# A four-stage graph network on one core: the two graph convolutions with a ring of 24 tile groups and loops over two step groups

## The reference, cut to what matters

```python
def gcn_conv(x, src, dst, W, b, n_nodes):
    deg = jax.ops.segment_sum(ones, dst, num_segments=n_nodes)
    dinv = jnp.where(deg > 0, jax.lax.rsqrt(jnp.maximum(deg, 1.0)), 0.0)
    norm = dinv[src] * dinv[dst]
    h = x @ W
    out = jax.ops.segment_sum(h[src] * norm[:, None], dst, num_segments=n_nodes)
    return out + b
h = jax.nn.relu(gcn_conv(x, src, dst, W1, b1, n))
return gcn_conv(h, src, dst, W2, b2, n)
```

## Time and profile before

| | us |
|---|---|
| median of three runs | 15079.31 |
| profiled execution | 14940.95 |
| its span | 14939.1 |
| first layer | 0 to about 3,300 |
| second layer | about 3,400 to 7,500 |
| third layer | about 7,600 to 10,130 |
| convolution 0, loops | 10209.5 to 12523 |
| convolution 1, loops | 12552 to 14861 |

### The profile page before, as it was taken

The page is one execution under the profiler, slowest core; times in us unless marked ns, Lnnn a source line. Parts: engine busy times, 40 slices in busy tenths (PEclk is TensorE's granted clock), DMA queues, the critical chain, the costliest instruction groups (busy, mean ns, idle before and its releaser), DMA issues.

```text
span 14939.1 us, 182194 instructions
## 1 busy us (share of the span) xinstructions
PE 8307.1 (56%) x46670; PEld 7582.8 (51%) x46671; DVE 6695.0 (45%) x13205; ACT 2723.1 (18%) x6542; POOL 8996.6 (60%) x8046
## 2 busy tenths in 40 slices
PE   5777787765555555578845555563333334333334
PEld 5777777754445444477745554463333333333333
DVE  6444444434444444489945565564222223222223
ACT  0111111101111111266623333340000000000000
POOL 3888888873556655500037777754666664666664
PEclk7666666666666667799967677775555555555555
DMA  4333333332333333332212222221111111111111
GB/s 91 18 18 18 18 18 18 18 51 68 97 96 98 98 99 96 99 100 98 94 47 66 66 68 67 67 65 27 23 23 23 23 23 26 23 23 23 23 23 23
DMA packets 851085, 769.36 MB, mean 51 GB/s; under 512 B 652784, under 2 KB 660804, under 8 KB 848965
## 3 DMA queue, kind: packets, MB, share of 16 engines
q0 software_dynamic: 446272, 333.87, 16.1%
q1 hardware_dynamic: 249485, 294.83, 5.9%
q10 hardware_dynamic: 155282, 140.11, 3.1%
HBM read 569.49 MB, written 197.82 MB: 51 GB/s over the span
## 4 chain that ended last, share of the span: by engine, by line
issue 23%; another core or an unknown queue 19%; PE 18%; POOL 15%; DVE 10%; DMA 8%; DVEq 5%; ACT 1%; ACTq 0%; POOLq 0%; SPq 0%
POOL lane_tab L679 9%; DMA lane_tab<-rows,idx 7%; POOL tab L703 6%; PE ps L1127 3%; PE ps L1153 3%; PE ps L1128 3%; DVEq L469 2%; DVE acc_w L1797 2%; DVEq L458 1%; DVE buf_d L469 1%; PE ps L1192 1%; PE ps L1178 1%; PE ps L1168 1%; PE ps L1113 1%
## 5 line engine op out<-in xcount | busy, mean ns | idle before, releaser
L703 POOL DMA_INDIRECT tab<-gcn_tab,idx x3136 | 2983.1, 951 | 1807.3 <-issue 1232.9
L679 POOL DMA_INDIRECT lane_tab<-rows,idx x1664 | 2598.3, 1561 | 616.8 <-issue 616.8
L703 POOL DMA_INDIRECT tab<-att_tab,idx x1568 | 1739.2, 1109 | 1923.1 <-DVEq L1684 1311.1
L1168 PE MATMUL ps<-tab,buf_d 128*128 x3328 | 795.2, 387 | 2162.6 <-issue 2121.8
L1168 PEld LDWEIGHTS ps<-tab,buf_d 128*128 128x128 f32 x3328 | 781.0, 320 | 2249.3 <-issue 2249.3
L1797 DVE TENSOR_TENSOR acc_w<-acc_w,ps 128x512 f32 x416 | 286.1, 688 | 3395.9 <-remote 3108.7
L693 POOL DMA_INDIRECT buf_b<-src_tab,idx x832 | 825.6, 992 | 749.4 <-ACT idx L813 296.4
L693 POOL DMA_INDIRECT acc_w<-src_tab,idx x832 | 838.0, 1007 | 598.0 <-ACT idx L813 335.1
L1065 PE MATMUL ps<-ident,srcg 128*128 128x128 f32 x3328 | 721.9, 405 | 659.6 <-DVE srcg L1430 655.1
L1168 PE MATMUL ps<-tab,buf_a 128*128 x3328 | 762.8, 424 | 531.7 <-issue 403.3
L1168 PEld LDWEIGHTS ps<-tab,buf_a 128*128 128x128 f32 x3328 | 725.9, 330 | 650.5 <-issue 650.1
(11 more groups left out here) (283 smaller groups left out, 16942.2 us busy)
## 6 DMA issues: line engine op xcount, KB each, us to landing
y_stash<-buf_c SPq DMA_DIRECT2D x208, 512.0 KB
tab<-y_stash SPq DMA_DIRECT2D x208, 512.0 KB, 3.3
aux<-dst_rows ACTq DMA_DIRECT2D x104, 512.0 KB
buf_b<-dst_rows ACTq DMA_DIRECT2D x104, 512.0 KB
tab<-gcn_tab,idx POOLq DMA_INDIRECT x3136
aux<-in_edge_attr_dram ACTq DMA_DIRECT2D x848, 32.0 KB
aux<-in_edge_attr_dram SPq DMA_DIRECT2D x848, 32.0 KB
lane_tab<-rows,idx POOLq DMA_INDIRECT x1664
```

The costliest lines, as they stand in the source:

```text
L679: pool.indirect_dma_start(lane_tab[k][:, :], bass.IndirectOffsetOnAxis(ap=idx[:, b, u:u + 1], axis=0), rows[:, b, u, 0:D1], None, compute_ ...
L703: pool.indirect_dma_start(to[k][:, u, :], None, table[:, :], bass.IndirectOffsetOnAxis(ap=idx[:, k % RING, u:u + 1], axis=0)).then_inc(row ...
L1168: last = pe.matmul(ps_flat[:, bass.ds(rel[u] + q * 512, D)], g_hot[q][:, u, :], g_ring[:, bass.ds(at[u], D)], start=False, stop=True, skip ...
```

## The change

The ring gets 24 slots (so AHEAD becomes 24 - 13 = 11). 24 slots of 512 floats fill most of `tab`, so the places move to `buf_b` in a shorter form (nine integers a step group: eight ring places and the needed tile groups), and the eight places in PSUM are read from `rel_s`, which is scaled in place. TensorE then loads registers twice a step group (`load8` and the new `load_tiles`). A ring of 24 is no power of two, so the place in the ring is worked out by VectorE with a multiplication, a shift and a multiply-add on the row `g_turn` in `buf_c`. Both loops run 104 times (ITER) over two step groups, with two one-hots and two banks. VectorE's order within a turn changes: it waits for the sum of step group g, adds it, frees the bank, and only then writes the one-hot of step group g + 2 into the buffer that step group g has just left. GpSimd's loop body becomes 24 tile groups long.

```diff
-LONG = 16
+LONG = 24
...
-        g_places = tab_flat[0:1, PLACES_AT:PLACES_AT + S // G * GP].bitcast(I32)
-        g_hot = [buf_a[:, 0, :, :], buf_a[:, 1, :, :], buf_d[:, 0, :, :], buf_d[:, 1, :, :]]
+        g_places = buf_b[:, :, :, :].rearrange("p a b c -> p (a b c)")[0:1, 0:S // G * (G + 1)].bitcast(I32)
+        g_turn = buf_c[:, :, :, :].rearrange("p a b c -> p (a b c)")[0:1, 0:S].bitcast(I32)
+        g_hot = [buf_a[:, 0, :, :], buf_a[:, 1, :, :]]
...
+        def load_tiles(g):
+            _, v = nc.values_load_multi_w_load_instructions(
+                g_places[:, bass.ds(g * (G + 1), G + 1)], engines=(mybir.EngineType.PE,), min_val=0, max_val=(LONG * G - 1) * D,
+                skip_runtime_bounds_check_because=PLACES_WHY)
+            return v[0:G], nc.s_assert_within(v[G], RING + 1, RING * (TT + 1))
...
             def aggregate(left_ready, landed, free, done):
-                with pe.Fori(0, TURNS) as i:
-                    for q in range(RING):
-                        g = i * RING + q
+                with pe.Fori(0, ITER) as i:
+                    for q in range(2):
+                        g = i * 2 + q
...
-                        rel, at, needed = load_steps(g)
+                        rel = load8(mybir.EngineType.PE, rel_s, g, (G - 1) * D)
+                        at, needed = load_tiles(g)
...
-            link(dve.tensor_scalar(row_s[:, 0:S], row_s[:, 0:S], LONG * G - 1, None, ALU.bitwise_and))
-            link(dve.tensor_scalar(g_steps[:, :, G:2 * G], row_grp, float(D), None, ALU.mult))
-            link(dve.tensor_scalar(g_steps[:, :, 0:G], rel_grp, float(D) / P, None, ALU.mult))
+            link(dve.tensor_scalar(g_turn, row_s[:, 0:S], 683.0, None, ALU.mult))
+            link(dve.tensor_scalar(g_turn, g_turn, 17, None, ALU.arith_shift_right))
+            link(dve.scalar_tensor_tensor(g_turn, g_turn, -float(LONG * G), row_s[:, 0:S], ALU.mult, ALU.add))
+            link(dve.tensor_scalar(g_steps[:, :, 0:G], g_turn.rearrange("p (a u) -> p a u", u=G), float(D), None, ALU.mult))
+            link(dve.tensor_scalar(rel_s[:, 0:S], rel_s[:, 0:S], float(D) / P, None, ALU.mult))
...
-                dve.sem_inc(bank_free, RING)
+                dve.sem_inc(bank_free, 2)
                 dve.sem_inc(outs, AHEAD)
                 for g in range(2):
                     one_hot_by_step(dve, g_hot[g], g).then_inc(hot, 1)
-                with dve.Fori(0, TURNS) as i:
-                    for q in range(RING):
-                        g = i * RING + q
-                        dve.wait_ge(outs, g + (AHEAD - 1))
-                        one_hot_by_step(dve, g_hot[(q + 2) % RING], g + 2).then_inc(hot, 1)
+                with dve.Fori(0, ITER) as i:
+                    for q in range(2):
+                        g = i * 2 + q
                         w0 = load1(mybir.EngineType.DVE, win_s, g, W - 1)
                         dve.wait_ge(outs, g + (AHEAD + 1))
                         a = acc_w[:, bass.ds(w0, G), 0:D]
...
                         dve.wait_ge(order, g + 2)
                         dve.sem_inc(bank_free, 1)
+                        one_hot_by_step(dve, g_hot[q], g + 2).then_inc(hot, 1)
```

More of the change, by code:

```diff
@@ L64 @@
 GP = 2 * G + 1
-PLACES_AT = LONG * G * D2
 ZEROS = 195
@@ L69 @@
 EPS = 1e-5
-assert 0 < AHEAD and LREST == RING and L2_RING % RING == 0 and all((t * 1639) >> 18 == t // (L2_RING * G) for t in range(T8)) and L2_RING * G * D2 + S <= 2 * W * D and 2 * G * P + S // G * GP <= W * D1 and PLACES_AT + S // G * GP + 2 * P <= 2 * W * D and WPP * PAIRS == W and LONG * G == P and TURNS * RING * G == S and SPAD == S + RING * G and SB == TB and CHUNKS * WPC == W and PAIRS * WPP == W and CHUNKS % 2 == 0 and ITER % 2 == 0 and ITER * PAIR == S and CH <= 512 and SROWS * D1 // P % ZEROS == 0
+assert 0 < AHEAD and LREST == RING and L2_RING % RING == 0 and all((t * 1639) >> 18 == t // (L2_RING * G) for t in range(T8)) and L2_RING * G * D2 + S <= 2 * W * D and 2 * G * P + S // G * GP <= W * D1 and LONG * G * D + P <= 2 * W * D and S // G * (G + 1) <= 2 * G * P and all((t * 683) >> 17 == t // (LONG * G) for t in range(T8)) and WPP * PAIRS == W and TURNS * RING * G == S and SPAD == S + RING * G and SB == TB and CHUNKS * WPC == W and PAIRS * WPP == W and CHUNKS % 2 == 0 and ITER % 2 == 0 and ITER * PAIR == S and CH <= 512 and SROWS * D1 // P % ZEROS == 0
 def build(nc, x, src, dst, ea16, ea64, w_edge, b_edge, w_node, b_node,
@@ L434, in build, with load_steps @@
         PLACES_WHY = "the table's entries are made from clamped step places"
-        def load_steps(g, places=g_places, stride=P // 2, n=D, ring=LONG):
+        def load_tiles(g):
[3 more added lines that the diff above has]
+            return v[0:G], nc.s_assert_within(v[G], RING + 1, RING * (TT + 1))
+        def load_steps(g, places, stride, n, ring):
             _, v = nc.values_load_multi_w_load_instructions(
@@ L1647, in _ @@
             dve.sem_inc(s.l2_windows, 1)
-            l2_steps, g_steps = (t.rearrange("p (a k) -> p a k", k=GP) for t in (l2_places, g_places))
+            l2_steps = l2_places.rearrange("p (a k) -> p a k", k=GP)
+            g_steps = g_places.rearrange("p (a k) -> p a k", k=G + 1)
             row_grp = row_s[:, 0:S].rearrange("p (a u) -> p a u", u=G)
@@ L1652, in needed_tiles @@
             def needed_tiles(steps):
-                needed = steps[:, :, 2 * G:GP]
+                n = steps.shape[2]
+                needed = steps[:, :, n - 1:n]
                 link(dve.tensor_scalar(needed, row_grp[:, :, G - 1:G], G.bit_length() - 1, None, ALU.arith_shift_right))
```

## The result

The changed kernel takes 15186.7 us (median of 9 runs, 15122.4 to 15211.2), the kernel before, measured beside it, 15077.1 us (9 runs, 15020.0 to 15083.6). The recorded ratio is 1.0086, 95% interval 1.0070 to 1.0102. That is a small loss, clear of the noise, where a gain was forecast (14420 us). The quotient of the two medians would be 1.0073. The ratios in this text are the recorded ones, and they can differ from the quotient of the medians by up to 0.3%. The profiled execution after has a span of 15184.8 us, 246 us above the one before, where the medians show 110 us. The stages say where the time lies.

A forecast was written before the change was run, and what follows sets the result against it. GpSimd's gathers and pauses were taken to bound the convolutions. 14941 - 668 (573 of it pauses) + 2 = 14275 us, plus 138 us from profiled execution to median, 14413, rounded to 14420 us; range 14380 to 15290 us.

The forecast's parts named there:

- What bounds the kernel: In the convolutions GpSimd always either gathers, one per 1.252 us, 1963 us a convolution, or pauses, 287 us.
- The ring of 24 as the gain: GpSimd's lead grows to 11 groups, 110 us of gathers, outlasting the 31.5 us hand-over delay; 573 us of pauses go.
- The third layer: Earlier stage with as many gathers, lead of seven groups, only 122.2 us of pauses; evidence against gathering itself slowing the hand-over.
- The tail: After a convolution's last gather: TensorE has only one or two step groups left, 14 us in place of 69.5.
- Two register loads: TensorE's second load per step group adds 1.4 us, making 7.2 us, hidden by the 10.0 us of a tile group.
- Two banks and two one-hots: TensorE's hand-over to VectorE in the convolutions may be 10 us late at no cost; delays of 19 and 31 uncovered.
- Rival D: Two banks lock TensorE to the gathering-dependent delay: three groups a turn, 35.8 us, +196 us, 15275 us; chance 0.32.
- Loop turns and setup: 104 more taken branches in the convolution loops cost zero; setup's three row operations become five, +2 us.
- A: The forecast itself: convolution hand-over delay does not grow, GpSimd gathers without pause; 14420 us, chance 0.40.

The follow-up runs named there:

- e1: Kernel before with the ring of 24 alone, with its table and second register load; 13329.7 us, ratio 0.9988, session without pauses.
- e4: Changed kernel with a GpSimd wait, before each tile group's fourth gather, for the previous tile group's rows; 13343.2 us, ratio 0.9996, session without pauses.
- e10: Changed kernel (ring of 24) with six banks, six one-hots and loops over six step groups; 14977.1 us, ratio 1.0042, session with pauses.
- e3: Kernel before with a GpSimd wait, before each tile group's fourth gather, for the previous tile group's rows; 13333.7 us, ratio 0.9987, session without pauses.
- e11: Kernel before with loops over two step groups, two one-hots and two banks alone, ring of 16; 14957.2 us, ratio 1.0041, session with pauses.
- e5: The changed kernel, unmodified, measured again beside the kernel before; 15038.6 us, ratio 1.0110, session with pauses.
- e7: Kernel before with loops over two step groups, two one-hots and two banks alone, same kernel as e2; ratio 1.0005, session without pauses.
- e2: Kernel before with loops over two step groups, two one-hots and two banks alone, ring of 16; 13337.6 us, ratio 0.9990, session without pauses.
- e13: Kernel before with a step group's one-hots written by one 128x1024 VectorE operation instead of eight; 13423.3 us, ratio 1.0050, session without pauses.
- e14: Kernel before with GpSimd waiting, ahead of each tile group, for the previous one's rows; ratio 1.0584, session without pauses.
- e16: Kernel before with GpSimd waiting, ahead of every second tile group, for the previous one's rows; ratio 1.0304, session without pauses.
- e17: Same kernel as e16, in a session of its own, also without pauses; ratio 1.0321.

## Why the prediction was wrong, point by point

**What bounds the kernel: right.** GpSimd either gathers at 1.25 us or pauses. In the sessions without pauses the gathers of a convolution take 1962 to 1971 us in e1 to e4, against the 1963 of the sum.

**The ring of 24 as the gain: the step that failed.** The sentence was "If delays stay of that size, GpSimd never waits", and it took 573 us off the time; 637 us of pauses in the two convolutions are what the changed kernel has (320 + 317), where the kernel before has 570. It took the hand-over delay of 31.5 us as a length of time that a lead of 110 us outlasts. The runs with pauses show a delay without a length: of the additions that the turn hangs on, the last comes only when GpSimd has been silent for four to five and a half us (medians: 5.3 with a lead of 3, 4.4 in the changed kernel and 5.4 in e10 with a lead of 11), however far GpSimd is ahead. The lead is spent once, in the first 14 tile groups, and then every turn ends in a pause again: 62 and 61 pauses in the changed kernel, 47 a convolution in e10 with the same ring. The forecast read the earlier trace rows, where the addition starts "when GpSimd has been silent for about five us", and did not let it decide. The third layer, the row that spoke against it, was the wrong witness. Fewer pauses of GpSimd there say nothing of how late the counts come to the other engines. Two lines of the kernel before for that stage (7645 to 10130 us), which the earlier trace rows does not show, say that they come late there too; the third line is the same place of VectorE in e3 (6959 to 9162 us), without pauses:

```profile
ACT buf_d L901 <- remote: 739.5, 56, 105.0
DVE buf_c L1713 <- remote: 523.2, 30, 61.0
```

```profile
DVE buf_c L1720 <- PE ps L1244: 450.5, 138, 15.3
```

GpSimd's 21 pauses of the third layer (130 us) are gone in e3 and e1 as well, and its gathers take 2200 and 2204 us there in place of 2351.

**The tail: wrong in its sign.** I took 14 us for it in place of 69.5, since TensorE would follow the data. With pauses TensorE follows up to eleven tile groups behind, and has them all to do after the last gather: 137 us to the next convolution's first gather in place of 99.5, with six banks and the ring of 24 118, with the ring of 16 and two banks (e11) 113. Both halves of the change lengthen the tail, the ring somewhat more. Without pauses the stretch is 36 us (e1).

**Two register loads: too dear.** I took 7.2 us a step group. In the changed kernel's tail the matmuls of consecutive groups start at 12599.79, 12605.99, 12611.44, 12616.44 and 12620.52:

```profile
12599.79 3.67 PE L1175 MATMUL ps<-tab,buf_a 128*128 x16
...
12605.99 3.67 PE L1175 MATMUL ps<-tab,buf_a 128*128 x16 [2.09 <-issue]
...
12611.44 3.67 PE L1175 MATMUL ps<-tab,buf_a 128*128 x16 [1.36 <-issue]
...
12616.44 3.67 PE L1175 MATMUL ps<-tab,buf_a 128*128 x16 [0.90 <-issue]
...
12620.52 3.67 PE L1175 MATMUL ps<-tab,buf_a 128*128 x16
```

That is 20.73 / 4 = 5.2 us a group, as before over four groups (12480.33 to 12501.17 us, 20.84 / 4), where the forecast had 5.8: the loads of nine integers take 2.35 us (median) where that of 17 took 4.03, and the loads of eight 0.59 us.

```profile
L437 PEldq TENSOR_LOAD <-buf_b x416: 1021/2352/2368, 10292.5 to 15099.7; - x139
```

**Two banks and two one-hots: right as a mechanism, and it decided.** Rival D had named it with the right place (TensorE's clearing matmul waiting for VectorE), the right point (a delay above 10 us; 20.4 us are seen) and the right count (three groups a turn). Its price a tile group was 11.95 us, measured 34.75 / 3 = 11.58, since the pause is 5.0 us and takes the place of one gap of 0.3: 3 x 10.0 + 4.7 against the 35.8 written. The larger error is the pause, which D took as long as before. Against 11.46 before that is 0.12 x 392 = 47 us where D had 196; in e11, which has this part alone, the gathers show 2 x 16 us. D left out the longer tail, 2 x 38 us, of which e11 shows 2 x 12. The whole change has a ratio of 1.0086, and 1.0110 in e5; the loops alone have 1.0041, the ring with six banks 1.0042. That the two halves about add up is no proof, since the ring with four banks was never measured with pauses and each interval is wide.

**Loop turns and setup:** nothing in the rows speaks against the zero and the 2 us; e7 and e2, with twice the turns and no pauses, are within 0.3% of before.

**Chances.** D had 0.32 and A 0.40. The range of 14380 to 15290 us holds the 15187 measured, but only because it was drawn to take in the nearer half of D; the forecast itself has the wrong sign and is 767 us too low. What should have turned them round is that the earlier trace rows show the same late addition at the same distance from GpSimd's last gather in turns of different content, while A rested on an analogy with another layer.

**What stays open.** Why the counts and TensorE's matmuls are held back while GpSimd gathers, and only in some sessions, is not settled. Neither a longer lead (e10, the changed kernel) nor more than four banks and one-hots (e10) removes it. Whether fewer instructions or short silences would free them was not seen, since e13, e14, e16 and e17 fell in sessions without pauses, nor whether a shorter queue of gathers would (e3, e4); what the ring alone does with pauses is known only from the change and from e10. No version measured beats both kernels in both kinds of session: with prompt counts all variants of ring, loops and banks are equal within 0.3%, with late ones the kernel before is the fastest of the four that were measured.

## What to carry to other kernels

Ask of a late hand-over what ends it before you buy slack against it: if each one ends at a fixed distance from another engine's silence, a longer lead only moves the silence, and lengthens the tail. When an engine's results are seen late, count the buffers between it and its reader first: two banks and two one-hots fewer turned four groups a turn into three here. And measure beside the old kernel in more than one session: a difference that one session shows can be nothing in another.

## What the runs showed of the hardware

The same kernel took 14890 to 15080 us in some sessions and 13320 to 13380 us in others at the same granted TensorE clock (0.64 to 0.65 as a mean over the span). In the convolutions the difference is whether counts of finished groups are seen at once (e1: VectorE's addition behind the matmuls, no "remote" wait of GpSimd) or late (by 20.4 us in the changed kernel's turn above, by 31.5 us in the earlier trace rows). But the convolutions and what follows hold only 669 of the 1614 us between the trace of the kernel before and that of e3, which is the same kernel with one wait more and without pauses. The largest part lies in the second layer, which the change does not touch: its gathers take 2799 us with 96 pauses (629 us) before, and 2168 us without any in e3.

In the late kind TensorE issues single matmuls 2.8 us apart, with "issue" between them, until GpSimd has been silent for about five us (the kernel before and e10). GpSimd's own gathers run at 0.95 us in both kinds. A VectorE operation of 128x1024 with two tensor inputs lengthened the gathers: those that overlapped it took 1060 ns on average in e13 and the others 943, which is 22 ns a gather over all of them, 69 us in all.
